# The score products between the second and the third value product of each block of an attention kernel

## What is computed

```
xs = reshape(_gn(x), (16, 1024, 512))
q, k, v = xs @ Wq[h], xs @ Wk[h], xs @ Wv[h]        # h = 0..7, 64 channels each
att = softmax(q @ k^T * 64**-0.5)
out = concat_h(att @ v) @ Wproj + bproj
return x + reshape(out, x.shape)
```

## Time and profile before

| | us |
|---|---|
| median of 3 runs | 4452.45 |
| lowest and highest run | 4452.08, 4463.26 |
| the profiled execution's own time | 4452.18 |
| its span | 4450.4 |
| PE busy in it | 4410.9 |
| POOL busy | 2857.7 |
| ACT busy | 2952.8 |
| DVE busy | 2580.5 |

### The profile page before, as it was taken

How to read it: one execution, slowest core, us unless ns; L and a number is a source line. 1 busy time by engine, 2 the same in 40 slices (tenths; PEclk the granted TensorE clock), 3 DMA queues, 4 the chain that set the end, 5 groups by cost and what they waited for, 6 DMA issues and landing times.

```text
span 4450.4 us, 61770 instructions
## 1 busy us (share of the span) xinstructions
PE 4410.9 (99%) x20864; PEld 3611.6 (81%) x20864; DVE 2580.5 (58%) x5063; ACT 2952.8 (66%) x5644; POOL 2857.7 (64%) x2227
## 2 busy tenths in 40 slices
PE   8999999999999999999999999999999999999999
PEld 7888888888888888888888888887888888888886
DVE  6655646556465565655656556565664656646454
ACT  5766757667576675756757567575775757757575
POOL 5666666666666566665666656666666666567566
PEclk9999999999999999999999999999999999999999
DMA  3111121211111112111121111211112111121201
GB/s 78 38 53 49 37 61 34 57 45 38 59 37 58 43 35 64 36 60 39 33 70 35 56 39 34 68 38 55 38 33 68 39 57 36 36 66 38 59 25 56
DMA packets 156825, 211.42 MB, mean 48 GB/s; under 512 B 56544, under 2 KB 57568, under 8 KB 156512
## 3 DMA queue, kind: packets, MB, share of 16 engines
q1 hardware_dynamic: 156512, 207.47, 16.5%
HBM read 105.12 MB, written 34.08 MB: 31 GB/s over the span
## 4 chain that ended last, share of the span: by engine, by line
PE 94%; DVE 2%; POOL 1%; ACT 1%; DMA 1%; issue 0%; SPq 0%; POOLq 0%; ACTq 0%; DVEq 0%
PE bank L663 16%; PE bank L715 10%; PE bank L881 10%; PE bank L882 10%; PE bank L883 10%; PE bank L709 10%; PE bank L708 10%; PE bank L675 8%; PE bank L693 8%; PE bank L681 1%; POOL prob_l L1294 1%; PE bank L700 1%; DVE smax L1106 1%; DVE xs L1073 0%; ACT prob L899 0%
## 5 line engine op out<-in xcount | busy, mean ns | idle before, releaser
L1294 POOL TENSOR_TENSOR prob_l<-prob,prob_h 128x512 fp32r<-128x512 f32 x1660 | 2140.5, 1297 | 1437.9 <-ACT prob_h L899 1418.2
L1106 DVE TENSOR_REDUCE smax<-bank 128x1 f32<-128x512 f32 x2048 | 1347.5, 682 | 868.2 <-PE bank L715 864.1
L899 ACT ACTIVATE prob<-bank 128x512 f32<-128x512 f32 x2048 | 1232.2, 602 | 575.3 <-PE bank L709 413.1
L899 ACT ACTIVATE prob_h<-bank 128x512 fp32r<-128x512 f32 x2048 | 1227.2, 599 | 461.9 <-PE bank L883 393.0
L881 PE MATMUL bank<-prob_h,vh 128*128 128x512 f32 x2048 | 822.2, 401 | 7.8 <-ACT acc L1018 4.2
L708 PE MATMUL bank<-q_hh,k_hl 128*128 128x512 f32 x2048 | 813.1, 397 | 0.0
L709 PE MATMUL bank<-q_lm,k_h 65*128 65x512 f32 x2048 | 811.4, 396 | 0.0
L882 PE MATMUL bank<-prob_h,vl 128*128 128x512 f32 x2048 | 806.3, 394 | 0.0
L883 PE MATMUL bank<-prob_l,vh 128*128 128x512 f32 x2048 | 805.8, 393 | 0.0
L715 PE MATMUL bank<-k_hl,q_hh 128*128 128x512 f32 x2048 | 716.4, 402 | 6.2 <-DVE smax L1106 6.0
L881 PEld LDWEIGHTS bank<-prob_h,vh 128*128 128x128 f32 x2048 | 388.8, 190 | 109.8 <-ACT acc L1018 15.4
(11 more groups left out here) (83 smaller groups left out, 5064.6 us busy)
## 6 DMA issues: line engine op xcount, KB each, us to landing
xs<-in_x SPq DMA_DIRECT2D x252, 256.0 KB, 2.8
q_hh<-q_hh SPq DMA_DIRECT2D x256, 128.0 KB, 2.2
k_hl<-k_h SPq DMA_DIRECT2D x256, 128.0 KB, 2.3
inv_b<-inv_dram SPq DMA_DIRECT2D x256, 128.0 KB, 2.8
out_x<-xs SPq DMA_DIRECT2D x128, 256.0 KB, 2.0
q_lm<-q_lm SPq DMA_DIRECT2D x256, 2.0 KB
den<-acc SPq DMA_DIRECT2D x256, 2.0 KB, 1.7
inv_dram<-inv SPq DMA_DIRECT2D x256, 2.0 KB, 1.4
```

Source lines behind the costliest of these rows:

```text
L899: return nc.scalar.activation(out, ps[ST + bank][:, :], ACT.Exp, scale=SCALE)
L1106: nc.vector.tensor_reduce(smax[:, 2 * t + half:2 * t + half + 1], ps[SM + turn][:, :], AX.X, ALU.max).then_inc(rows_used, 1)
L1294: nc.gpsimd.tensor_tensor(prob_l[:, r3, :], prob[:, ring2, :], prob_h[:, r3, :].bitcast(F32), ALU.subtract).then_inc(prob_l_pool, 1)
```

## The change

The order within a block of TensorE becomes: first side work; the waits for `acc_ready`, the values and, new at this place, `prob_h` of block i; the first two value products; the two score products of block i + 3, with their waits as before; the wait for the low part; the third value product; second side work. So the score products (and not the side work, which now stands at the block's beginning) are between the second and the third value product. No instruction is added or taken away on any engine.

```
             for i in range(BLOCKS):
+                    other_work(s, i, 0)
+
+                    tc, t = divmod(i, TT)
+                    pair = s.h // 2
+                    if t == 0 and not (first and tc == 0):
+
+                        pe.wait_ge(acc_ready, s.heads(2, 0, tc))
...
+                    pe.wait_ge(prob_h_ready, s.heads(BLOCKS, 0, i + 1))
+                    ring = ring3(s, i)
...
+                    nc.tensor.matmul(ps[bank][:, :], v_hi_op, prob_h[:, ring, :], start=t == 0, stop=False)
+                    nc.tensor.matmul(ps[bank][:, :], v_lo_op, prob_h[:, ring, :], start=False, stop=False)
                     ahead, j = divmod(i + AHEAD, BLOCKS)
                     if not (end and ahead):
                         def wait():
...
                         scores((s.k + ahead) % 2, j, ring3(s, i + AHEAD), wait)
-                    other_work(s, i, 0)
...
-                        pe.wait_ge(acc_ready, s.heads(2, 0, tc))
...
                     lo_wait(pe, s, i)
-                    ring = ring3(s, i)
...
-                    nc.tensor.matmul(ps[bank][:, :], v_hi_op, prob_h[:, ring, :], start=t == 0, stop=False)
-                    nc.tensor.matmul(ps[bank][:, :], v_lo_op, prob_h[:, ring, :], start=False, stop=False)
                     nc.tensor.matmul(ps[bank][:, :], v_hi_op, prob_l[:, ring, :],
                                      start=False, stop=t == TT - 1).then_inc(pv_done, 1)
                     other_work(s, i, 1)
```

More of the change, by code:

```diff
@@ L850, in step @@
                 for i in range(BLOCKS):
[L852 to L860, removed]
                     other_work(s, i, 0)
@@ L875, in step @@
                             entry_taken(pe, s, "v", 4 + t // 2, back=3 - t // 4)
-                    lo_wait(pe, s, i)
+                    pe.wait_ge(prob_h_ready, s.heads(BLOCKS, 0, i + 1))
                     ring = ring3(s, i)
@@ L882, in step, with wait @@
                     nc.tensor.matmul(ps[bank][:, :], v_lo_op, prob_h[:, ring, :], start=False, stop=False)
+                    ahead, j = divmod(i + AHEAD, BLOCKS)
+                    if not (end and ahead):
+                        def wait():
+                            pe.wait_ge(prob_h_ready, s.heads(BLOCKS, 0, i + 1))
+                            if j == 0:
+                                pe.wait_ge(mrow_in[0], s.heads(16, 1, 16))
+                            if j == TT:
+                                pe.wait_ge(mrow_in[1], s.heads(16, 0, 16))
+                        scores((s.k + ahead) % 2, j, ring3(s, i + AHEAD), wait)
+                    lo_wait(pe, s, i)
                     nc.tensor.matmul(ps[bank][:, :], v_hi_op, prob_l[:, ring, :],
```

## The result

| | before | changed |
|---|---|---|
| median, us | 4452.26 (4 runs) | 4535.0 (4 runs) |
| lowest and highest | 4449.39, 4463.26 | 4533.62, 4536.9 |
| profiled execution: span, us | 4450.4 | 4531.8 |

The ratio is 1.0182, with a 95% interval of 1.0167 to 1.0197: the changed kernel is 1.8% slower. The spans differ by 81.4 us, and the granted clock is 1.0 after and 0.999 before.

The account below looks back on a forecast made before the run. It took TensorE's queue (busy 99%, 94% of the chain) as the bound; 5.69 us a pass times 15 gave 85, plus 4 for other heads, less 6: +83 on 4452.2, so 4535 us, range 4495 to 4565, 8 times in 10.

Parts of the forecast that it names:

- the signs named beforehand: In the changed profile: copy wait from 15 to some 60 us, maxima wait up some 20, low part's wait gone.
- 0.46 us of cover: On TensorE, two score products no longer cover the wait for PVB's copy: 0.46 us at a boundary that waits already.
- 0.26 of lateness: On ScalarE, the copy out of PVB starts 0.69 instead of 0.43 us after the third value product: 0.26 us later.
- ScalarE falls behind at each of the 16 boundaries of a pass: Rival, chance 0.08: three ScalarE instructions in a row cost another 0.26 us per boundary, 62 us more, 4597 us.
- The steps costed at nothing: Repeated wait for `prob_h` and PSUM bank switches within the value products: taken as zero, bounded by 0.11 us a step.
- The distance of 0.17 us from a releaser's end to the waiter: At TensorE's waits: 0.06 us to start plus 0.11 for a held weight load; a distance d has d - 0.17 to spare.
- the places with little to spare: Head 6 block 8: 0.52 us; start of head 4: 0.35; block 8 of heads 1, 2 and start of head 5: 0.06 each.
- Those of heads 6 and 7: Row scores at block 11, waiting for maxima or their copy: 0.46 us in head 6, 0.40 in head 7, per pass.
- the two of block 9: Row scores in heads 4 and 5 waiting for the last row score's maximum: 0.32 us each per pass.
- The bullets: The list of TensorE places that lose time in one pass of eight heads, summing to 5.69 us.
- I take 6: Gain from the low part's waits going: 6 us of at most 9, the wait coming 0.92 us later in TensorE's queue.
- The rule against the change: Trainium skill's bank rotation advice: the single PVB bank's copy loses the scores beside it, 0.72 us a place.

Follow-up runs that it names:

- t0_only: Against lo_late: score products after the second value product in blocks 0 and 8 only, first elsewhere; 4507.26 us.
- t7_only: Against lo_late: score products after the second value product in blocks 7 and 15 only; runs from 4463.46 to 4481.21 us, 7 us over its forecast of 4465.
- after_copy_first: Against the changed kernel: ScalarE's copy out of PVB placed before the exponential in blocks 7 and 15; 4517.19 us, ratio to the kernel before 1.0144.
- lo_late: Against the kernel before: only the low part's wait moves, to directly before the third value product; scores stay first; 4455.03 us against 4453.3, ratio 1.0004.
- middle_only: Against lo_late: score products after the second value product in all blocks but 0, 7, 8 and 15; 14 us over its forecast of 4476 us.
- words: Against the changed kernel: first side work moved behind the score products, both between the second and third value product; 4629.65 us, ratio to the kernel before 1.0395.
- before_rows: Against the kernel before: two row scores of head 6 block 11 moved from first to second side work; 4470.31 us against 4453.03, ratio 1.0038.

## Why the prediction was right

**The bound.** That the kernel lasts as long as TensorE's queue, and that the moved wait could win under 10 us, held: 5 us of waits vanished. Of the signs named beforehand, the wait for the copy grew to 79.5 us (some 60 were expected), that for the maxima by 16.5 (some 20), and that for the low part fell to 2.6 and is not quite gone.

**The terms of a boundary.** 0.46 us of cover and 0.26 of lateness were read from different rows, and t0_only (0.46), t7_only (0.25) and after_copy_first (the lateness gone, 0.46 left) show each by itself. That ScalarE falls behind at each of the 16 boundaries of a pass did not come: the starts of heads 1, 2, 3 and 5 cost less than 0.05 us each. The steps costed at nothing held too: over all blocks L873 to L708 is 0.231 us in the mean and L709 to L884 0.234. (L709 is 65 rows deep, as its rows say, and not 128 as told further up; its step is 0.23 us all the same.) The distance of 0.17 us from a releaser's end to the waiter is confirmed at the places with little to spare: 0.519 measured for 0.52, 0.341 for 0.35, 0.043 for 0.06.

**The row scores.** Those of heads 6 and 7 are within 0.02 us of the forecast; the two of block 9 are 0.36 and 0.35 for 0.32. In the changed kernel, answering to the earlier trace rows:

```profile
2505.27 0.69 DVE L1107 TENSOR_REDUCE smax<-bank 128x1 f32<-128x512 f32 x1
...
2506.02 0.82 PE L715 MATMUL bank<-k_hl,q_hh 128*128 128x512 f32 x2 [0.68 <-DVE smax L1107]
```

```profile
2547.17 1.12 PE L715 MATMUL bank<-k_hl,q_hh 128*128 128x512 f32 x2
2547.45 0.28 DVE L1118 CAST q_lm<-bank 4x128 fp32r<-4x128 f32 x1 [0.39 <-PE bank L700]
```

The idle time grew from 0.20 to 0.68 us at the first; at the second the two row scores, 0.63 us before, take 1.12 with the wait between them.

**What was wrong in the sum and cancelled.** The bullets left out head 4 block 4 (4.0 us in all) and the relief at head 6 block 13 and head 7 block 3 (6.7 us in all), and the term "I take 6" for the low part is at most 4: lo_late gains 1.8 us at head 6 block 9 and 0.4 in the last head, and nothing in the total. That term was also worked out wrongly. Counted from the end of the block before, the wait passes two matmuls more than it did and not four, so it comes 0.46 us later and not 0.92, against a low part that is 0.26 later.

The relief is no steady gain. The kernel before has both stalls in the same 4 of its 15 passes, which lose 0.97 and 0.74 us by them, and none in the 11 others, though all passes have the same instructions; the changed kernel has them in none. Its stalls at the heads' starts are not the reason at head 6 block 13: middle_only lacks those stalls and has the relief there (-0.23), and t0_only has most of them and no relief (+0.05). What decides in which passes a stall comes is not shown.

So the places do not simply add up: the parts measured alone, 54 us for t0_only, 19 for t7_only and 36 for middle_only, make 109 against the changed kernel's 82. I was right to 1 us in a total in which single terms missed by 4 to 7, and part of that is luck.

**The rule against the change.** Rotating banks so that the evacuation of a group runs beside other matmuls (the Trainium skill, Perfetto Trace Analysis, Optimizing Tensor Performance, Matmuls) was the right warning: with the single bank PVB, all that hides its copy is other groups' work, and words shows 1.2 us lost at a head's start when that work is gone.

**Left open.** Why the row scores of block 9 cost 0.36 and not 0.32 us was not pursued. At head 6 block 13 and head 7 block 3, which of GpSimd's instructions lengthens the normalisation was read in one pass each of before_rows, after_copy_first and the changed kernel only. Why equal passes differ there stays open.

## What to carry to other kernels

Before an instruction is moved in a full queue, ask not what it waits for but what waits it covers where it stands: here 0.46 us of score products hid a copy, a maximum and their latencies at a dozen places, and the wait that was moved had been free almost everywhere. A table of the distance from releaser to waiter at each place, less the 0.17 us that a release needs, gave every term foreseen to 0.04 us. And a wait taken away can start another engine's work beside a third's: add up places only if the queues behind them keep their order and their neighbours.

## What the runs showed that I had not expected

VectorE's `tensor_scalar` on a 128x512 tile in SBUF takes 0.53 to 0.55 us while GpSimd is idle and up to 1.59 us beside GpSimd's subtraction of 1.29 us. In the trace of before, the 14 that overlap no instruction of GpSimd last 528 to 546 ns; of the 102 that lie beside GpSimd's instructions for more than half of their time the median is 919 and the longest 1593 ns. Of the 33 that start within 0.4 us behind the start of one of GpSimd's, 32 end 0.28 to 0.29 us after that one's end, whatever its length. VectorE's maxima from PSUM do not change: 681 ns in the median beside GpSimd, at most 694 with it and without. Three in a row took 2.72 us or 4.30 us, according to whether GpSimd paused (above). This fits what the Trainium skill says (SBUF — State Buffer, SBUF: two separate sides): VectorE and GpSimd share a port pair which is locked, not divided; an instruction of VectorE in a two-port mode that comes second waits until GpSimd's whole instruction is done, and the other way round. The runs show VectorE's waiting; the lock itself, and the mode in which `tensor_scalar` ran, they do not show. The waiting made 18 us of difference in t0_only, where GpSimd starts 0.13 us ahead of the first normalisation (2420.15, 2420.28) instead of 0.74 (2387.30, 2388.04), so that its pause falls elsewhere.
